# Sign network: ±1 weights of two layers in bf16, their inputs split into three bf16 parts

## The reference

```python
def _conn_dense(kernel_bool, x):
    w = jnp.where(kernel_bool, jnp.float32(1.0), jnp.float32(-1.0))
    return x @ w
h = jnp.concatenate([x, -x], axis=-1)       # [4096, 256]
h = s0 * _conn_dense(k0, h)                 # k0: 256 x 512
h = jax.nn.relu(h) * 2
h = s1 * _conn_dense(k1, h)                 # k1: 512 x 512
h = jax.nn.relu(h) * 2
h = s2 * _conn_dense(k2, h)                 # k2: 512 x 128
```

## Time and profile before

| what | value |
|---|---|
| time, median of 3 runs | 2993.87 us (2988.32 to 3002.89) |
| span of the profiled execution, first to last instruction | 2977.2 us |
| PE busy in it | 2648.4 us (89%) |
| DVE, ACT, POOL busy | 1981.0, 1625.1, 491.0 us (67, 55, 16%) |
| `sign_mlp`: first product to end of the last L1100 | 2796.57 to 2967.27, 170.7 us |

### The profile page before, as it was taken

One profiled execution on the slowest core, in us unless ns is written; L12 is line 12 of the kernel. 1 busy time (PEld: TensorE's weight loads), 2 busy tenths in 40 slices (PEclk: granted clock), 3 DMA queues, 4 the chain that ended last, 5 costly groups with the idle time before them and its releaser, 6 DMA issues. The chain is left out here.

```text
span 2977.2 us, 72656 instructions
## 1 busy us (share of the span) xinstructions
PE 2648.4 (89%) x21433; PEld 1793.4 (60%) x21433; DVE 1981.0 (67%) x4869; ACT 1625.1 (55%) x3951; POOL 491.0 (16%) x1072
## 2 busy tenths in 40 slices
PE   5999999977899896666999999999999976999898
PEld 4888888854566553433666666666666654666454
DVE  5666666654688646755878888887787755888311
ACT  3555555532577622223777777777777753666310
POOL 2111111100122100001222222222222202332000
PEclk9999999978799986766999999999999997999899
DMA  3000000000222100002222222222222211222001
GB/s 127 1 0 0 0 0 0 0 1 4 72 76 72 37 1 0 0 0 60 73 75 71 74 72 75 71 75 70 75 72 74 70 34 54 71 70 66 1 0 28
DMA packets 123330, 128.37 MB, mean 43 GB/s; under 512 B 17402, under 2 KB 102222, under 8 KB 123215
## 3 DMA queue, kind: packets, MB, share of 16 engines
q1 hardware_dynamic: 123214, 126.94, 15.5%
HBM read 85.36 MB, written 39.88 MB: 42 GB/s over the span
## 5 line engine op out<-in xcount | busy, mean ns | idle before, releaser
L631 DVE TENSOR_REDUCE a_rowmax<-a_psS 128x2 f32<-128x512 f32 x1536 | 995.9, 685 | 284.7 <-PE a_psS L443 261.8
L561 ACT ACTIVATE a_probs<-a_psT 128x512 f32<-128x512 f32 x1536 | 882.4, 595 | 315.8 <-PE a_psT L455 287.8
L443 PE MATMUL a_psS<-stackk,stackq 65*128 65x256 bf16 x3072 | 607.4, 280 | 85.6 <-DMA stackk<-mask_dram 39.2
L455 PE MATMUL a_psT<-stackq,stackk 98*128 98x256 bf16 x3072 | 593.5, 275 | 17.0 <-ACT a_probs L561 5.5
L443 PEld LDWEIGHTS a_psS<-stackk,stackq 65*128 65x128 bf16 x3072 | 237.1, 98 | 316.2 <-DVE a_rowmax L631 188.2
L469 PE MATMUL a_psO<-a_probs,values 128*32 128x256 f32 x6144 | 414.4, 387 | 0.0
L455 PEld LDWEIGHTS a_psT<-stackq,stackk 98*128 98x128 bf16 x3072 | 275.7, 98 | 117.3 <-ACT a_probs L561 53.4
L469 PEld LDWEIGHTS a_psO<-a_probs,values 128*32 128x32 f32 x6144 | 161.0, 109 | 148.3 <-issue 72.9
L730 POOL TENSOR_SCALAR a_negmax<-a_rowmax 128x16 bf16<-128x16 f32 x192 | 48.5, 252 | 983.6 <-DVE a_rowmax L631 983.6
L900 ACT ACTIVATE a_probs<-a_psS,a_negmax 128x256 f32<-128x256 f32 x256 | 120.4, 470 | 158.8 <-DVE a_negmax L925 158.8
L949 DVE TENSOR_SCALAR a_kT<-a_psQ,l_bqk 64x256 f32<-64x256 f32 x256 | 123.7, 483 | 78.8 <-ACT a_qT L893 76.9
(11 more groups left out here) (195 smaller groups left out, 4405.8 us busy)
## 6 DMA issues: line engine op xcount, KB each, us to landing
a_scratch<-a_parts SPq DMA_DIRECT2D x96, 384.0 KB, 2.8
stackq<-a_scratch SPq DMA_DIRECT2D x192, 96.0 KB
stackk<-a_scratch SPq DMA_DIRECT2D x192, 96.0 KB
stackq<-a_scratch SPq DMA_DIRECT2D x192, 64.0 KB
stackk<-a_scratch SPq DMA_DIRECT2D x192, 64.0 KB
stackq<-a_scratch SPq DMA_DIRECT2D x192, 32.0 KB
stackk<-a_scratch SPq DMA_DIRECT2D x192, 32.0 KB
stackq<-a_negmaxT SPq DMA_DIRECT2D x384, 4.0 KB
```

What stands on the lines that cost most here:

```text
L443: mm = pe.matmul(psS[h % 2][:, t * SEQ:(t + 1) * SEQ], stackq[0:MASK_ROW + 1, b, h, t * P:(t + 1) * P], stackk[0:MASK_ROW + 1, b, h, :], s ...
L455: mm = pe.matmul(psT[h % 2][:, t * SEQ:(t + 1) * SEQ], stackk[0:MAX_ROW + 2, b, h, t * P:(t + 1) * P], stackq[0:MAX_ROW + 2, b, h, :], sta ...
L561: act.activation(probs[:, h // 4 % 2, h % 4, :], psT[h % 2][:, :], ACT.Exp, scale=w.exp_scale).then_inc(exp_done, 1)
L631: dve.tensor_reduce(rowmax[:, s.parity(1), h, :], psS[h % 2][:, :].rearrange("p (t k) -> p t k", t=2), AX_X, ALU.max).then_inc(max_done, 1)
```

## The change

k0 and k1 are made as bf16 (their entries are exact in it). Each operand that moves against them is split into three bf16 parts that sum to the fp32 value: the value rounded to bf16, the remainder rounded to bf16, and the remainder of that. Each fp32 product becomes three bf16 products with the same weights, added up in the same PSUM bank. k2 and its product out(g) stay in fp32.

The split of h0 takes five steps for each (g,c): ACT writes the rounded relu to `h0p[..,0]` and the same relu in fp32 to `whole0` (two activations from the bank, in place of one); DVE subtracts the first from the second in place ("rest"); POOL copies the rest to bf16, `h0p[..,1]` ("middle"); DVE subtracts that into `h0p[..,2]` ("low"), and this last one raises `h0_ready`. `whole0` has two buffers, by the parity of c. The same is done with each group of x, two steps ahead: ACT copies x to `xp[..,0]`, DVE subtracts in place in `m.xT8`, POOL copies, DVE subtracts; the last raises `x_ready`, for which a(g,0) waits. The stage has 14 semaphores, before 6.

```diff
@@ -1040,11 +1040,15 @@
     CH = FF3 // P
     with ExitStack() as ctx:
         sem, sb, begin = stage(nc, ctx, "mlp")
-        h0 = sb("h0", [P, 2, CH, 512])
+        xp = sb("xp", [P, 2, 3, 512], BF16)
+        h0p = sb("h0p", [P, 2, CH, 3, 512], BF16)
+        whole0 = sb("whole0", [P, 2, 512])
         h1 = sb("h1", [P, CH, 512])
         pb = lambda n: ctx.enter_context(nc.psum_tensor(f"mlp_{n}", [P, 512], F32))
         banks0, banks1, out = [pb("a0"), pb("a1")], [pb("b0"), pb("b1")], [pb("out0"), pb("out1")]
-        p0, h0_ready, p1, h1_ready, out_ready, x_updated = (sem("p0"), sem("h0_ready"), sem("p1"), sem("h1_ready"), sem("out_ready"), sem("x_updated"))
+        x_high, x_rested, x_middle, x_ready = sem("x_high"), sem("x_rested"), sem("x_middle"), sem("x_ready")
+        p0, whole0_ready, rest0_ready, middle0, h0_ready = sem("p0"), sem("whole0_ready"), sem("rest0_ready"), sem("middle0"), sem("h0_ready")
+        p1, h1_ready, out_ready, x_updated, pool_passed = sem("p1"), sem("h1_ready"), sem("out_ready"), sem("x_updated"), sem("pool_passed")
         block = begin()
 
         plan = Plan(jobs=GROUPS, weights=1, unroll=2, first=2, rounds=(GROUPS - 4) // 2, drain=1)
@@ -1054,9 +1058,14 @@
             def step(s):
                 for c in range(CH):
                     if s.has(1):
+                        if c == 0:
+                            pe.wait_ge(x_ready, s.n(1, 1, 1))
                         if s.known(1, 1) or c >= 2:
-                            pe.wait_ge(h0_ready, s.n(1, CH, c - 1))
-                        pe.matmul(banks0[c % 2][:, :], w.k0[:, c * P:(c + 1) * P], m.xT8[:, s.batch(1), :], start=True, stop=True).then_inc(p0, 1)
+                            pe.wait_ge(whole0_ready, s.n(1, CH, c - 1))
+                        for part in range(3):
+                            mm = pe.matmul(banks0[c % 2][:, :], w.k0[:, c * P:(c + 1) * P], xp[:, s.parity(1), part, :],
+                                           start=(part == 0), stop=(part == 2))
+                        mm.then_inc(p0, 1)
                     if c == 1 and s.has(-1):
                         pe.wait_ge(h1_ready, s.n(-1, CH, CH))
                         if s.known(-1, 2):
@@ -1072,8 +1081,9 @@
                         if s.known(0, 1) or c >= 2:
                             pe.wait_ge(h1_ready, s.n(0, CH, c - 1))
                         for k in range(CH):
-                            mm = pe.matmul(banks1[c % 2][:, :], w.k1[:, k, c * P:(c + 1) * P], h0[:, s.parity(0), k, :],
-                                           start=(k == 0), stop=(k == CH - 1))
+                            for part in range(3):
+                                mm = pe.matmul(banks1[c % 2][:, :], w.k1[:, k, c * P:(c + 1) * P], h0p[:, s.parity(0), k, part, :],
+                                               start=(k == 0 and part == 0), stop=(k == CH - 1 and part == 2))
                         mm.then_inc(p1, 1)
 
             pipeline(pe, plan, step)
@@ -1082,13 +1092,33 @@
         def _(act):
             def step(s):
                 for c in range(CH):
+                    if c == 0 and s.has(2):
+                        if s.known(2, 2):
+                            act.wait_ge(p0, s.n(0, CH, CH))
+                        act.activation(xp[:, s.parity(2), 0, :], m.xT8[:, s.batch(2), :], ACT.Copy).then_inc(x_high, 1)
                     if s.has(1):
                         act.wait_ge(p0, s.n(1, CH, c + 1))
                         if c == 0 and s.known(1, 2):
                             act.wait_ge(p1, s.n(1, CH, -CH))
-                        act.activation(h0[:, s.parity(1), c, :], banks0[c % 2][:, :], ACT.Relu, scale=w.s[:, 0:1]).then_inc(h0_ready, 1)
+                        if s.known(1, 1) or c >= 2:
+                            act.wait_ge(h0_ready, s.n(1, CH, c - 1))
+                        act.activation(h0p[:, s.parity(1), c, 0, :], banks0[c % 2][:, :], ACT.Relu, scale=w.s[:, 0:1])
+                        act.activation(whole0[:, c % 2, :], banks0[c % 2][:, :], ACT.Relu, scale=w.s[:, 0:1]).then_inc(whole0_ready, 1)
 
             pipeline(act, plan, step)
+
+        @block.gpsimd
+        def _(pool):
+            def step(s):
+                for c in range(CH):
+                    if s.has(1):
+                        wait_alone(pool, rest0_ready, s.n(1, CH, c + 1), pool_passed)
+                        pool.tensor_copy(h0p[:, s.parity(1), c, 1, :], whole0[:, c % 2, :]).then_inc(middle0, 1)
+                    if c == 1 and s.has(2):
+                        wait_alone(pool, x_rested, s.n(2, 1, 1), pool_passed)
+                        pool.tensor_copy(xp[:, s.parity(2), 1, :], m.xT8[:, s.batch(2), :]).then_inc(x_middle, 1)
+
+            pipeline(pool, plan, step)
 
         @block.vector
         def _(dve):
@@ -1099,11 +1129,24 @@
                         dve.wait_ge(out_ready, s.n(-1, 1, 1))
                         dve.scalar_tensor_tensor(out=m.xg[:, g, :], in0=out[s.parity(-1)][:, :], scalar=w.s[:, 2:3], in1=m.xg[:, g, :],
                                                  op0=ALU.mult, op1=ALU.add).then_inc(x_updated, 1)
+                    if s.has(1):
+                        dve.wait_ge(whole0_ready, s.n(1, CH, c + 1))
+                        dve.tensor_tensor(whole0[:, c % 2, :], whole0[:, c % 2, :], h0p[:, s.parity(1), c, 0, :], ALU.subtract).then_inc(rest0_ready, 1)
+                    if c == 1 and s.has(2):
+                        dve.wait_ge(x_high, s.n(2, 1, 1))
+                        dve.tensor_tensor(m.xT8[:, s.batch(2), :], m.xT8[:, s.batch(2), :], xp[:, s.parity(2), 0, :], ALU.subtract).then_inc(x_rested, 1)
                     if s.has(0):
                         dve.wait_ge(p1, s.n(0, CH, c + 1))
                         if c == 0 and s.known(0, 1):
                             dve.wait_ge(out_ready, s.n(0))
                         dve.tensor_scalar(h1[:, c, :], banks1[c % 2][:, :], w.s[:, 1:2], 0.0, ALU.mult, ALU.max).then_inc(h1_ready, 1)
+                    if s.has(1):
+                        dve.wait_ge(middle0, s.n(1, CH, c + 1))
+                        dve.tensor_tensor(h0p[:, s.parity(1), c, 2, :], whole0[:, c % 2, :], h0p[:, s.parity(1), c, 1, :],
+                                          ALU.subtract).then_inc(h0_ready, 1)
+                    if c == 2 and s.has(2):
+                        dve.wait_ge(x_middle, s.n(2, 1, 1))
+                        dve.tensor_tensor(xp[:, s.parity(2), 2, :], m.xT8[:, s.batch(2), :], xp[:, s.parity(2), 1, :], ALU.subtract).then_inc(x_ready, 1)
 
             pipeline(dve, plan, step)
 
@@ -1483,7 +1526,7 @@
 
     ku = [held("k0_bytes", [P, 2, FF3 // 4], a["k0"], I32)[:, :, :].bitcast(U8), held("k1_bytes", [P, 4, FF3 // 4], a["k1"], I32)[:, :, :].bitcast(U8),
           held("k2_bytes", [P, 4, D // 4], a["k2"], I32)[:, :, :].bitcast(U8)]
-    mlp = W(k0=sb("k0", [P, FF3]), k1=sb("k1", [P, 4, FF3]), k2=sb("k2", [P, 4, D]), s=sb("s", [P, 3]))
+    mlp = W(k0=sb("k0", [P, FF3], BF16), k1=sb("k1", [P, 4, FF3], BF16), k2=sb("k2", [P, 4, D]), s=sb("s", [P, 3]))
     s_in = held("s_in", [P, 3], bcast(a["s"], 3))
 
     m.l0_loaded, m.rest_loaded = ctx.enter_context(nc.semaphore("l0_loaded")), ctx.enter_context(nc.semaphore("rest_loaded"))
```

## The result

| | median of the runs | ratio to before | 95% interval |
|---|---|---|---|
| before | 2993.87 us (2988.32 to 3002.89, 7 runs) | | |
| after | 2982.30 us (2973.16 to 2984.71, 7 runs) | 0.9948 | 0.993 to 0.9965 |
| after, a second time, beside further runs of before (2985.39 us) | 2970.61 us (12 runs) | 0.9951 | 0.9934 to 0.9967 |

The change makes the kernel 0.5% faster; 2980.9 was forecast. The ratio 0.9948 is 15.6 us, where the two medians differ by 11.6. The single executions of either kernel in the first two rows are spread over 12 to 15 us, so it takes the changed stage itself to say which of the two is the change.

What follows compares the result with a forecast made beforehand. PE was taken to bound the final stage. Opening +9.0, products -32.6, boundaries +7.7, low clock +2.5 and semaphores +0.4 sum to -13.0 us, taking 2993.87 to 2980.9 us; range 2973 to 2992.

Steps and rivals of the forecast that it cites:

- What bounds the kernel: PE bounds the last stage, `sign_mlp`, without a gap between groups; its gains come out at the end one for one.
- The sum: All terms together: -13.0 us, stage 157.3 us, span 2964.2 us, time 2980.9 us, 0.43% less.
- The product: On PE, a bf16 product of 512 tokens takes 0.216 us; three make 0.648, saving 0.210 us per fp32 product.
- The boundary: Between groups PE waits for relu and low part: about 1.0 us six times, 1.65 at g = 7, +7.7 us.
- DVE's slack: From the end of out until b(g,3) ends, DVE has 8.5 us of work in 9.1, leaving 0.6 us.
- The port: DVE subtractions and POOL casts lock shared SBUF ports; where they meet, at c = 1, one is 0.2 to 0.4 us later.
- The opening: At the stage's start, splitting x and h0 delays the first b from 7.0 to about 16.0 us: +9.0 us.
- The semaphores: Before the store, SP clears eight more semaphores at 0.05 us each: +0.4 us, at most 1.1.
- The low clock: From the first b, PE's clock stays low for about 5 us of products, half of that lost: +2.5 us.
- Rival (1): PE's clock rises early, during group 0's four a, and stays up, a product takes 0.2146 us: 2976.7 us; chance 0.28.

Runs made afterwards that it cites:

- two parts: The changed kernel, but PE multiplies only the high and middle parts and leaves out the low one, which DVE still makes; stage 148.9 us against 155.9.

## Why the prediction held

**What bounds the kernel** held. The stage is the tail of the program, and its 15.8 us come out at the end; both ratios say so. The sum gave the stage 13.4 us, 2.4 less than it gained. That the forecast of 2980.9 lies so near the median of 2982.30 is in part luck: by the ratio the time is 2978.3. And 0.5% is just where the prediction drew the line between a faster kernel (0.33) and no change (0.61), so these two chances can't be told apart by the result.

**The product** of 0.216 us held to the digit: twelve in 2.59 us.

**The boundary** held: 7.7 us were forecast. The trace has 6.4 us of PE waits, and seven tails of 0.17 us that the profile counts as busy make 7.6. Behind the first b PE waited nowhere else but ahead of the last out. That the low part stands behind the relu, and not POOL's cast or the port, is shown by two runs: swapping the two took 2.9 us off, and covering the low part with out took the wait for it away.

**DVE's slack** was put at 0.6 us; the trace after shows DVE idle 0.60 us ahead of the fourth relu of a group, and in group 1 another 0.36 ahead of the third. Two runs passed the slack, one by adding work on DVE and one by taking it from PE, and in both PE waited.

**The port**: the casts that meet a subtraction took 0.91 us instead of 0.61, and the low part behind them up to 1.07 instead of 0.69. It was forecast at c = 1, and there it is. The sizes fit whole waits and no sharing. In the rows above 0.43 us were left of the subtraction when the cast came, which took 0.30 more; 0.52 were left of x's cast when the low part came, which took 0.38 more. Both are 0.13 to 0.14 less than what was left by the profile, and so are the two of the earlier trace rows (0.16 of 0.30, 0.20 of 0.34). The Trainium skill has it so (SBUF — State Buffer, section "SBUF: two separate sides"): whichever of the two began first keeps the ports for its whole instruction, and the other stands still; the traces agree, with these numbers. That they wait for a port, and not for something else that they share, no run separates.

**The opening** held: first b 16.0 us into the stage, 15.6 measured, counted from the stage's first instruction (ACT's L1098). The fp32 start of group 0 shows that it is worth 6.4 us net.

**The semaphores** held: +0.4 forecast, 1.27 - 0.84 = +0.43 measured.

**The low clock was mis-sized.** "I take the clock to be low when b starts and to stay low for about 5 us of products" gave +2.5. It was 1.6 us of products and 0.8 us in the first trace, 4.4 us and 2.2 in the second. The clock rose at a moment that differed between two executions of the same program by 2.8 us. That makes the term a range, 0.8 to 2.2, and the forecast took the upper end. It is 1.7 of the 2.4 us between the stage that was forecast, 157.3 from its first instruction, and the first trace's 154.9; the opening, 8.5 us longer than before and not 9.0, is most of the rest. The second trace has 156.3. Rival (1) asked for a clock that rises in the opening and stays. It rose there, which the forecast did not say (0.50 until 5 us behind the first b), but fell again in the 5.6 us in which PE idles.

**One sentence was wrong**: that the median's 16.7 us above the span is "launch and completion". The profiled execution of after took 2982.72 us with a span of 2981.0, so it is 1.7 us. The profiled execution of before, whose device time is not listed, was then about 2979 us (its span and 1.7, an estimate), shorter than each of the seven listed runs; its masked attention was a short one among those traced. The sum was a difference, so the error cancelled.

## What to carry to other kernels

Splitting fp32 into bf16 parts pays 0.21 us on each product of 512 columns only where the making of the parts is hidden. Ask for the last part of each group, and what stands in front of it in its engine's order: here one relu and one subtraction cost 7.6 of the 33 us that the products saved, and moving one piece on PE gave 3.4 of it back (against the trace with the same clock). Price the first pass through a new chain of hand-overs by itself, since nothing covers it; if it costs more than the old way for one group, run that group the old way. And measure a tail stage between two of its own instructions, when the program ahead of it varies by more than the change.

## What the runs showed that was not expected

The clock's fall under waits of PE. Idle times of 0.8 to 1.4 us, once per group of 17.5 us, left it at 1.00 throughout. With three more subtractions on DVE, waits of 0.3 to 0.7 and of 1.3 us with a short run of products between left it there too, and so did a single one of 1.84 us at the last boundary. With two parts, waits of 0.9 to 1.7 us so placed, and at the end a single one of 2.45, brought it to 0.50 at every boundary. Half of what was lost there is the waits and half the clock, and together they cost 27 of the 34.5 us that had been taken off PE. So a cut of work on the bound engine can lose most of its worth to the clock as well as to the next engine, and here the waits for the one brought the other.
